# Two states of a Mamba scan take their inputs from GpSimd in SBUF and their decays from ScalarE in PSUM, without PE's transposes

## The chip, the cores and the metric

The kernel runs on one core of one Trainium2 chip. All arithmetic is float32. The metric is the device time of one execution in microseconds; the median of three runs counts, and a shorter time is better. The engines are called as the profile calls them: PE (TensorE matmuls; PEld are its weight loads), DVE (VectorE), ACT (ScalarE), POOL (GpSimd), SP (SyncE, which issues all DMAs here).

## The reference

The input x is (2, 2048, 256). It is normalised, and goes through a Mamba block and a gated feed-forward, each with a residual, then through a mixture of 8 low-rank experts of which the best 2 count. What matters here is the selective scan, with 512 inner channels d, 16 states s and 2048 positions t:

```python
dt = softplus(dt @ dt_proj_w.T + dt_proj_b);  A = -exp(A_log)
def step(h, t):
    dt_t, B_t, C_t, x_t = t
    dA = jnp.exp(dt_t[..., None] * A)
    h = h * dA + dt_t[..., None] * B_t[:, None, :] * x_t[..., None]
    y = jnp.einsum('bds,bs->bd', h, C_t)
    return (h, y)
```

For each state the scan needs a *decay* exp(dt[d,t]·A[d,s]) and an *input* u[d,t]·B[t,s], with u = dt·x. B and C are the same for all channels.

## The kernel before, in words

The sequence is cut into 8 chunks of 256 positions, and there are 2 batches, so the kernel takes 16 *steps* of (chunk, batch). A step passes through five stages, each split in 16 turns: **enter** (norm, input projection, convolution, B and C), **ready** (dt with its softplus, u = dt·x, transposes of u), **main** (the scan), **back** (gate, output projection, feed-forward) and **tail** (router and experts). In one pass of the loop five neighbouring steps are under way at once, each in another stage. The function `drive` writes this order for every engine: for each turn s = 0 to 15, `main(s, n, 0)`, then the turn of the other four stages, then `main(s, n, 1)`. All waits are explicit semaphores; each engine runs its program in order. Steps 0 and 1 have no back or tail beside them, the last one no enter or ready.

Turn s of `main` deals with state s in two halves of 256 channels:

- The input is made with positions on the partitions: `bxT` = uTs · B's column, where B is one scalar per partition. ACT makes it for eleven states (L795), POOL for states 4, 6, 8, 14 and 15 (L561), in a ring of three places, up to three turns ahead. The order of the ring and who must be done with a place are in `ring`, `ring_before` and `made_at`.
- PE turns it by transposes into one of three PSUM banks `psx` (`fill_bx`, L1241), one turn ahead. A bank is free when the scan of three halves earlier is done; the first two fills of the next step are issued in turn 15 of `ready`.
- ACT makes the decay `dA` in SBUF, four exponentials for each state (`decay`, L807), three turns ahead.
- DVE scans (L998): `h` from dA (SBUF) and psx (PSUM), and ACT keeps the last column in `state`.
- POOL multiplies h by C's row, which SP has spread over all partitions in `bC` (L577, `hC`). PE sums hC over the states in `psy`, two turns later, by accumulating transposes (L1260).

Around that, in the other stages: DVE's share of the softplus is L979 and L981 in turn 8 and L985 in turn 9 of `ready`. POOL adds dt (L549) in turn 9 and makes u (L553) in turn 10, in the place of sp_l. In turn 9 of `enter` POOL finishes the convolution (L541), ACT makes xc from it (L708). The second gate (L820) comes in turn 10. The tail's expert sums are the matmuls L1123 from `w_b_sb` into `pst`; turn 14 has sixteen of them in the profile, and DVE adds the result in turn 15 (L1092), between the two halves of state 15's scan. SP stores the expert weights cT and loads them back spread over the partitions (`cbc`), in turn 5 of `tail`; DVE uses them from turn 7 on (L1073).

Of the kernel before, what the change touches and what calls it, by code (L numbers as in the profile page):

```python
# [28 lines left out]
POOL_STATES = (4, 6, 8, 14, 15)  # L29
# [64 lines left out]
def made_at(s):  # L94

    return (-2, -1)[s] if s < 2 else s - 3 if s < S - 1 else S - 3
# [86 lines left out]
def mamba_moe(nc, x, params, w_in, w_x, w_dt, w_out, w_ff, w_fo, w_a, w_b, w_r, bc_scratch, cw_scratch, out):  # L183
# [9 lines left out]
    with ctx:  # L193
# [43 lines left out]
        low = sb("low", [P, T])  # L237
        bc = sb("bc", [2 * S, T])
        sp_e = sb("sp_e", [P, NJ, T])
        sp_l = sb("sp_l", [P, NJ, T])  # L240
        dt = sb("dt", [P, B, NJ, T])
# [35 lines left out]
        cT = sb("cT", [NE, T])  # L277
# [6 lines left out]
        u = sp_l  # L284
        hg = yg
        sk = acc

# [33 lines left out]
        exp_done, scan_done, state_saved = sem("exp_done"), sem("scan_done"), sem("state_saved")  # L321
        hc_done, skip_added, y_summed = sem("hc_done"), sem("skip_added"), sem("y_summed")
# [57 lines left out]
        def _(sp):  # L380
# [23 lines left out]
            def load_c(m, g, multiplied):  # L404

                sp.wait_ge(hc_done, multiplied)
                sp.dma_start(bC[:, g % RINGG], bc_scratch[m[1]][g * G:(g + 1) * G, :].partition_broadcast(P)
                             ).then_inc(c_loaded[g % RINGG], 16)

            def enter(s, m):  # L410
                if s == 7 and not is_last(m):
                    load_x(following(m))
                if s == 13:

                    spread, made = value(count(16 * NG // RINGG, m, -16 * NG // RINGG)), value(count(1, m, 1))
                    for i in range(RINGG):
                        sp.wait_ge(c_loaded[i], spread)
                    sp.wait_ge(bc_done, made)
                    sp.dma_start(bc_scratch[m[1]], bc[S:2 * S, :]).then_inc(bc_stored, 16)
# [28 lines left out]
            def tail(s, m):  # L448
                if s == 5 and not is_last(m):
# [5 lines left out]
                    sp.dma_start(cw_scratch, cT[:, :]).then_inc(cw_stored, 16)  # L455
# [14 lines left out]
        def _(pool):  # L470
# [25 lines left out]
            def norm_again(m):  # L496

                turned, scaled = value(count(len(IN_UNITS), m, 1 - len(IN_UNITS))), value(count(1, m, 1))
                pool.wait_ge(ident_ready, 1)
# [44 lines left out]
            def ready(s, m):  # L544
# [5 lines left out]
                if s == 10:  # L550
                    pool.wait_ge(dt_done, count(1, m, 1))
                    pool.wait_ge(xc_done, count(1, m, 1))
                    nc.gpsimd.tensor_tensor(u[:, :, :], dt[:, b], xc[:, b], ALU.mult).then_inc(u_done, 1)  # L553

            def weigh_u(s, n):
# [4 lines left out]
                pool.wait_ge(bx_filled, count(FILLS, n, HALVES * (ring_before(s) + 1)))  # L560
                nc.gpsimd.tensor_tensor(bxT[:, ring(s)], uTs[:, n[1]],  # L561
                                        BT[:, n[1], :, s:s + 1].to_broadcast([P, SUB, DI]), ALU.mult
                                        ).then_inc(bxT_pool, 1)

            def main(s, n, part):
                if part == 0:
# [81 lines left out]
        def _(act):  # L648
# [70 lines left out]
            def ready(s, m):  # L719
                b = m[1]  # L720
                if s == 0:

                    act.wait_ge(filled_in, in_fill("low", m))
                    nc.scalar.activation(low[:, :], psf[:, 0, :], ACT.Copy).then_inc(low_done, 1)
                if s in (1, 2):

                    i = s - 1
                    act.wait_ge(sp_rest, count(1, m, 0))
                    act.wait_ge(filled_dt, dt_fill(f"dt{i}", m))
# [9 lines left out]
                if s == 6:  # L739

                    act.wait_ge(sp_exp, count(1, m, 1))
                    act.wait_ge(filled_dt, count(len(DT_UNITS), m, 0))
# [18 lines left out]
                if s in (13, 14):  # L761

                    j = s - 13
                    act.wait_ge(bxT_pool, count(len(POOL_STATES), m, -len(POOL_STATES)))
                    act.wait_ge(bxT_act, count(S - len(POOL_STATES), m, len(POOL_STATES) - S))
# [14 lines left out]
            def made(turn, n):  # L780

                for k in range(S):
                    if made_at(k) == turn and k not in POOL_STATES:
                        weigh_u(k, n)
                if turn + 3 < S and not (is_first(n) and turn < -1):
                    decay(turn + 3, n)

            def weigh_u(s, n):
# [4 lines left out]
                act.wait_ge(bx_filled, count(FILLS, n, HALVES * (ring_before(s) + 1)))  # L793
                for j in range(SUB):
                    last = nc.scalar.activation(bxT[:, ring(s), j, :], uTs[:, n[1], j, :], ACT.Copy,  # L795
# [14 lines left out]

            def keep_state(s, n):
# [10 lines left out]
            def main(s, n, part):  # L822
                if part == 0 and s == 3:
# [16 lines left out]
            def back(s, m):  # L840
# [10 lines left out]
                if s == 9:  # L851

                    act.wait_ge(filled_back, back_fill("vT", m))
# [589 lines left out]
```

## Time and profile before

| | |
|---|---|
| runs | 1322.29, 1322.62, 1326.65 us; median 1322.62 |
| profiled execution | 1323.98 us, its span 1322.3 us |
| granted TensorE clock over the span | 0.981 |
| busy | PE 93%, PEld 80%, DVE 76%, ACT 79%, POOL 82% |
| DMA | 74.02 MB, mean 56 GB/s |

The busy shares are means over the whole span; five stages with different needs lie side by side in it. Which engine is waited for has to be read from a stretch of one step. In the rows of the trace "[0.33 <-DVE h]" behind an instruction is the time that its engine was idle before it, and who ended that. Start times are us from the span's start.

### The profile page before, as it was taken

The numbers are of one execution on the slowest core, as the hardware profiler recorded it, in microseconds if no ns is written. First come the engines' busy times: TensorE is split into PE (matmuls) and PEld (weight loads), VectorE is DVE, ScalarE is ACT, GpSimd is POOL, SyncE is SP. The second block draws the span as 40 slices with busy tenths as digits, with TensorE's granted clock in tenths as the row PEclk, the third lists the DMA queues.
The fourth block names the chain that finished last, engine by engine and source line by source line (L and its number), as shares of the span: only waits on it lengthen the run. The fifth ranks groups of instructions, "written<-read, shape, count | busy, mean of one in ns | idle before, by whom it ended". The sixth has DMA issues, their size and how long they took to land.

```text
span 1322.3 us, 24291 instructions
## 1 busy us (share of the span) xinstructions
PE 1230.5 (93%) x7678; PEld 1053.4 (80%) x7678; DVE 1007.8 (76%) x1800; ACT 1039.6 (79%) x2506; POOL 1079.4 (82%) x820
## 2 busy tenths in 40 slices
PE   5677899999999999999999999999999999999988
PEld 3466778887888888788888878888887888887876
DVE  2597969788796977879697797968779796878633
ACT  4989988798787879878797887879788787878521
POOL 2589898998988888888898988889898888889721
PEclk8799999999999999999999999999999999999998
DMA  2411112021121202112111211211111121202010
GB/s 67 177 49 41 49 41 78 21 81 49 33 81 49 78 20 82 48 35 81 51 57 41 75 39 50 81 45 61 41 57 57 50 73 47 66 32 75 17 49 16
DMA packets 29063, 74.02 MB, mean 56 GB/s; under 512 B 3080, under 2 KB 15744, under 8 KB 26496
## 3 DMA queue, kind: packets, MB, share of 16 engines
q1 hardware_dynamic: 28928, 72.35, 16.4%
q8 instruction: 69, 1.13, 0.3%
q14 instruction: 66, 0.54, 0.1%
HBM read 63.56 MB, written 4.58 MB: 52 GB/s over the span
## 4 chain that ended last, share of the span: by engine, by line
PE 61%; DVE 15%; issue 9%; ACT 4%; POOL 2%; DMA 1%; DVEq 0%; SPq 0%; POOLq 0%; ACTq 0%
PE psx L1241 10%; PE psy L1260 10%; PE pst L1123 8%; PE psb L1123 8%; DVE h L998 8%; PE psb L1117 6%; PE psf L1117 4%; PE psf L1209 2%; PE psf L1160 2%; PE psf L1149 2%; PE psb L1215 2%; DVE acc L971 2%; DVE sp_l L985 1%; DVE cbc L1073 1%; PE psx L1117 1%
## 5 line engine op out<-in xcount | busy, mean ns | idle before, releaser
L998 DVE TENSOR_TENSOR_SCAN h<-dA,state,psx 128x256 f32<-128x256 f32 x1024 | 682.6, 726 | 112.4 <-PE psx L1241 96.3
L577 POOL TENSOR_TENSOR hC<-h,bC 128x1024 f32<-128x1024 f32 x256 | 607.0, 2378 | 81.5 <-DVE h L998 74.8
L807 ACT ACTIVATE dA<-dt,neg_a 128x256 f32<-128x256 f32 x1024 | 434.2, 500 | 0.0
L1241 PE MATMUL psx<-ident,bxT 128*128 128x128 f32 x2048 | 306.0, 275 | 29.0 <-DVE h L998 23.8
L1241 PEld LDWEIGHTS psx<-ident,bxT 128*128 128x128 f32 x2048 | 243.9, 142 | 75.5 <-issue 29.3
L795 ACT ACTIVATE bxT<-uTs,BT 128x512 f32<-128x512 f32 x352 | 232.6, 715 | 67.2 <-PE psx L1241 65.7
L1260 PE MATMUL psy<-ident,hC 128*128 128x128 f32 x2048 | 265.5, 273 | 1.4 <-POOL hC L577 1.4
L1260 PEld LDWEIGHTS psy<-ident,hC 128*128 128x128 f32 x2048 | 233.1, 142 | 4.7 <-POOL hC L577 1.7
L561 POOL TENSOR_TENSOR bxT<-uTs,BT 128x1024 f32<-128x1024 f32 x80 | 152.1, 1902 | 24.8 <-PE psx L1241 24.8
L1117 PE MATMUL psb<-nT,w_ff_sb 128*128 128x256 f32 x496 | 121.8, 388 | 15.1 <-ACT yg L820 13.5
L1117 PEld LDWEIGHTS psb<-nT,w_ff_sb 128*128 128x128 f32 x496 | 89.3, 190 | 37.0 <-ACT yg L820 19.7
L1123 PE MATMUL pst<-w_b_sb,cbc 128*128 128x256 f32 x480 | 110.8, 379 | 0.0
L1123 PEld LDWEIGHTS pst<-w_b_sb,cbc 128*128 128x128 f32 x480 | 90.1, 190 | 11.7
L971 DVE SCALAR_TENSOR_TENSOR acc<-psf,par,acc 128x255 f32<-128x255 f32 (+1 forms) x180 | 73.9, 474 | 22.6 <-ACT halo L703 22.6
L1117 PE MATMUL pst<-eT,w_a_sb 128*128 128x256 f32 x336 | 79.4, 379 | 0.0
L492 POOL TENSOR_SCALAR nx<-x,mv,rstd 128x256 f32<-128x256 f32 x60 | 72.9, 1225 | 0.0
L1117 PEld LDWEIGHTS pst<-eT,w_a_sb 128*128 128x128 f32 x336 | 61.7, 190 | 7.2
L1123 PE MATMUL psb<-w_out_sb,yg 128*128 128x256 f32 x256 | 63.6, 393 | 2.0 <-ACT yg L847 2.0
L1117 PE MATMUL psf<-uT,w_in_sb 128*128 128x256 f32 x240 | 60.2, 395 | 3.4 <-DVE acc L971 2.0
L549 POOL TENSOR_TENSOR dt<-dt,sp_l 128x1024 f32<-128x1024 f32 x16 | 37.8, 2364 | 28.0 <-DVE sp_l L985 28.0
L814 ACT ACTIVATE state<-h 128x4 f32<-128x4 f32 x256 | 50.5, 203 | 12.8 <-DVE h L998 12.8
L1123 PE MATMUL psb<-w_fo_sb,yg 128*128 128x256 f32 x256 | 60.4, 379 | 0.0
(168 smaller groups left out, 1641.4 us busy)
## 6 DMA issues: line engine op xcount, KB each, us to landing
bC<-bc_scratch SPq DMA_DIRECT2D x64, 512.0 KB, 3.9
cbc<-cw_scratch SPq DMA_DIRECT2D x15, 1024.0 KB, 4.7
xf<-in_x SPq DMA_DIRECT2D x16, 256.0 KB, 2.7
xk<-xn SPq DMA_DIRECT2D x16, 256.0 KB, 4.3
xb<-in_x SPq DMA_DIRECT2D x16, 256.0 KB, 4.3
out<-x SPq DMA_DIRECT2D x16, 256.0 KB, 2.2
w_in_sb<-in_w_in SPq DMA_DIRECT2D x1, 1024.0 KB, 5.4
w_ff_sb<-in_w_ff SPq DMA_DIRECT2D x1, 1024.0 KB, 5.8
```

What stands on the lines that cost most here:

```text
L492: last = nc.gpsimd.tensor_scalar(dst[:, j, :], src[:, j, :], mv[k][:, j, 0:1], rstd[k + 1][:, j:j + 1], ALU.subtract, ALU.mult)
L561: nc.gpsimd.tensor_tensor(bxT[:, ring(s)], uTs[:, n[1]], BT[:, n[1], :, s:s + 1].to_broadcast([P, SUB, DI]), ALU.mult).then_inc(bxT_pool, 1)
L577: nc.gpsimd.tensor_tensor(hC[:, s % RC], h[:, ring(s)], bC[:, g % RINGG, s % G:s % G + 1, :].to_broadcast([P, NJ, T]), ALU.mult).then_inc( ...
L795: last = nc.scalar.activation(bxT[:, ring(s), j, :], uTs[:, n[1], j, :], ACT.Copy, scale=BT[:, n[1], j, s:s + 1])
L807: last = nc.scalar.activation(dA[:, s % RA, j, :], dt[:, n[1], j, :], ACT.Exp, scale=neg_a[:, j, s:s + 1])
L814: nc.scalar.activation(state[:, n[1], :, s:s + 1], h[:, ring(s), :, T - 1:T], ACT.Copy).then_inc(state_saved, 1)
L971: nc.vector.scalar_tensor_tensor(out=acc[:, j, tap:], in0=x_bank(i, m)[:, j % 2, 0:T - tap], scalar=pcol(C_CONVW + j * TAPS + k), in1=acc[ ...
L998: last = nc.vector.tensor_tensor_scan(h[:, r, j, :], dA[:, s % RA, j, :], psx[bx_bank(fill)][:, k, :], state[:, b, j, s:s + 1], ALU.mult, ...
L1117: last = mm(dst[:, i, :], w[:, k, c:c + P], rhs[:, k, :], start=k == 0, stop=k == kt - 1)
L1123: last = mm(dst[:, j, :], lhs[:, k, j * P:(j + 1) * P], w[:, k, :], start=k == 0, stop=k == kt - 1)
L1241: last = nc.tensor.transpose(psx[bx_bank(fill)][:, k, j * P:(j + 1) * P], bxT[:, ring(s), j, c:c + P], ident[:, :])
L1260: last = mm(psy[j][:, i * P:(i + 1) * P], hC[:, s % RC, i, j * P:(j + 1) * P], ident[:, :], is_transpose=True, start=False, stop=s == S - ...
```

## The change

States 14 and 15 are called `DIRECT`. For them nothing is turned. POOL multiplies u (channels on the partitions) by B's row, spread over all partitions like C's, and leaves the input in SBUF. ACT writes the exponentials into the `psx` banks that PE filled before, in two groups of two for each state, and the scan reads its decays from PSUM and its inputs from SBUF. The order of POOL's products changes: those for 14 and 15 stand in turns 8 and 10 (`weigh_direct`), not in turns 11 and 13. SP stores B together with C in DRAM and loads the two rows in turn 5.

Places: the input of state 14 is made in `ygt`, that of state 15 in `sp_e`, B's rows lie in `un`; `u` gets a tile of its own in place of sp_l's; `low` and `cT` lie in the dead `nT`. Each of these sharings comes with waits, at the head of the instruction that writes the place. `bxT` now has fourteen states, so its ring is simply s % 3, and the first two bxT of a step need state 12's and 13's transposes only. In the diff, cut to its core, come the shared helpers and places, then SP, POOL (`norm_again`, `ready`, `weigh_u`, `weigh_direct`, `main`), ACT, DVE and PE.

```diff
-POOL_STATES = (4, 6, 8, 14, 15)
+DIRECT = (14, 15)
+POOL_STATES = (4, 6, 8)
+TURNED = HALVES * (S - ND)
...
-    return (-2, -1)[s] if s < 2 else s - 3 if s < S - 1 else S - 3
+    return (-2, -1)[s] if s < 2 else s - 3
...
+def turned_before(s):
+    return s - RX if s >= RX else (12, 13, 11)[s] - S
...
+def turned(s):
+    return HALVES * (s + 1) if s >= 0 else HALVES * (s + S + 1) - TURNED
...
-        u = sp_l
+        low = nT[:, 0, :]
+        cT = nT[0:NE, 1, :]
+        bB = un
+        def direct_inputs(s):
+            return (ygt[:, :, :].rearrange("p j (k t) -> p (j k) t", t=T), sp_e[:, :, :])[DIRECT.index(s)]
...
+                if part == 0 and s == 5:
+                    gone = value(count(len(IN_UNITS), n, 1 if is_late(n) else 2 * len(IN_UNITS) + 1))
+                    sp.wait_ge(filled_in, gone)
+                    sp.dma_start(bB[:, :, :], bc_scratch[n[1]][DIRECT[0]:DIRECT[0] + ND, :].partition_broadcast(P)
+                                 ).then_inc(b_loaded, 16)
...
+                pool.wait_ge(direct_done, weighed)
...
+                    pool.wait_ge(filled_dt, count(len(DT_UNITS), m, 0))
+                    pool.wait_ge(direct_done, count(ND, m, 0))
...
-                pool.wait_ge(bx_filled, count(FILLS, n, HALVES * (ring_before(s) + 1)))
+                pool.wait_ge(bx_filled, count(TURNED, n, turned(turned_before(s))))
+            def weigh_direct(i, n):
+                if i == 0:
+                    pool.wait_ge(b_loaded, count(16, n, 16))
+                    pool.wait_ge(u_done, count(1, n, 1))
+                    pool.wait_ge(filled_back, count(len(BACK_UNITS), n, 2 - len(BACK_UNITS)))
+                else:
+                    pool.wait_ge(sp_rest, count(1, n, 1 if is_last(n) else 2))
+                nc.gpsimd.tensor_tensor(direct_inputs(DIRECT[i]), u[:, :, :],
+                                        bB[:, i:i + 1, :].to_broadcast([P, NJ, T]), ALU.mult).then_inc(direct_done, 1)
             def main(s, n, part):
+                if part == 0 and s in (8, 10):
+                    weigh_direct((8, 10).index(s), n)
...
+            def decay_direct(s, part, n):
+                fill = HALVES * s + part
+                act.wait_ge(scan_done, count(FILLS, n, bx_before(fill) + 1))
+                for k in range(PAIR):
+                    j = PAIR * part + k
+                    last = nc.scalar.activation(psx[bx_bank(fill)][:, k, :], dt[:, n[1], j, :], ACT.Exp,
+                                                scale=neg_a[:, j, s:s + 1])
+                last.then_inc(direct_exp, 1)
             def main(s, n, part):
+                if s + 1 in DIRECT:
+                    decay_direct(s + 1, part, n)
...
+                if s in DIRECT:
+                    dve.wait_ge(direct_exp, count(HALVES * ND, n, fill - TURNED + 1))
...
+                    decays, inputs = ((in_psum, direct_inputs(s)[:, j, :]) if s in DIRECT
+                                      else (dA[:, s % RA, j, :], in_psum))
...
             def main(s, n, part):
-                if s + 1 < S:
+                if s + 1 < S - ND:
                     fill_bx(s + 1, part, n)
```

On PE, turns 12 to 15 of a steady step (psx0 to psx2 are the three banks; `MATMUL psy<-ident,hC` is the sum over states) are before:

```order
L1241 MATMUL psx1<-ident,bxT 128x128 x4
L1223 MATMUL psf<-ident,sp_l 128x128 x4
...
L1241 MATMUL psx2<-ident,bxT 128x128 x4
...
L1241 MATMUL psx0<-ident,bxT 128x128 x4
L1123 MATMUL pst<-w_b_sb,cbc 128x256 x8
...
L1241 MATMUL psx1<-ident,bxT 128x128 x4
...
L1241 MATMUL psx0<-ident,bxT 128x128 x4
L1241 MATMUL psx1<-ident,bxT 128x128 x4
L1160 MATMUL psf<-xc,w_x_sb 128x256 x4
```

And in the changed kernel the same stretch reads:

```order
L1300 MATMUL psf<-ident,u 128x128 x4
L1200 MATMUL psb<-w_fo_sb,yg 128x256 x4
L1200 MATMUL pst<-w_b_sb,cbc 128x256 x4
...
L1200 MATMUL pst<-w_b_sb,cbc 128x256 x8
...
L1318 MATMUL psx0<-ident,bxT 128x128 x4
L1318 MATMUL psx1<-ident,bxT 128x128 x4
L1237 MATMUL psf<-xc,w_x_sb 128x256 x4
```

Four psx groups are gone: three ahead of the end of the expert matmuls (`w_b_sb`, x8), one behind them. The last two psx groups are the next step's state 0.

On POOL, turns 7 to 10 of a steady step (`nx` is the back stage's norm, the hC are those of states 7, 8, 9 and 10) are before:

```order
L492 TENSOR_SCALAR nx<-x1,mv1,rstd2 128x256 x2
...
L577 TENSOR_TENSOR hC<-h,bC 128x1024
...
L577 TENSOR_TENSOR hC<-h,bC 128x1024
...
L549 TENSOR_TENSOR dt<-dt,sp_l 128x1024
...
L541 TENSOR_TENSOR acc<-acc,edge 128x4x3
...
L577 TENSOR_TENSOR hC<-h,bC 128x1024
L553 TENSOR_TENSOR sp_l<-dt,xc 128x1024
...
L577 TENSOR_TENSOR hC<-h,bC 128x1024
...
L561 TENSOR_TENSOR bxT<-uTs,BT 128x1024
```

And in the changed kernel:

```order
L626 TENSOR_TENSOR hC<-h,bC 128x1024
...
L609 TENSOR_TENSOR ygt<-u,un 128x1024
...
L626 TENSOR_TENSOR hC<-h,bC 128x1024
...
L583 TENSOR_TENSOR dt<-dt,sp_l 128x1024
...
L575 TENSOR_TENSOR acc<-acc,edge 128x4x3
...
L626 TENSOR_TENSOR hC<-h,bC 128x1024
L609 TENSOR_TENSOR sp_e<-u,un 128x1024
...
L589 TENSOR_TENSOR u<-dt,xc 128x1024
```

The product for state 14 (into ygt) now stands between the hC of state 7 and that of state 8, the one for state 15 (into sp_e) between the hC of state 9 and u; the bxT that stood behind the hC of state 10 is gone.

## Rows read from the trace of the kernel before

**Rows 1.** The page: busy time, the chain that ended last; and all of L1092.

```profile
PE 1230.5 (93%) x7678; PEld 1053.4 (80%) x7678; DVE 1007.8 (76%) x1800; ACT 1039.6 (79%) x2506; POOL 1079.4 (82%) x820
...
PE 61%; DVE 15%; issue 9%; ACT 4%; POOL 2%; DMA 1%; DVEq 0%; SPq 0%; POOLq 0%; ACTq 0%
...
L1092 DVE TENSOR_TENSOR x<-x,pst x15: 686/689/689, 263.9 to 1297.5; 128x512 f32<-128x512 f32 x15
```

**Rows 2.** PE in order of time, one steady step: start us, us, instruction.

```profile
705.27 1.99 PE L1117 MATMUL psb<-nT,w_ff_sb 128*128 128x256 f32 x8 [0.90 <-ACT yg L820]
...
725.21 0.60 PE L1241 MATMUL psx<-ident,bxT 128*128 128x128 f32 x4
725.64 3.62 PE L1123 MATMUL pst<-w_b_sb,cbc 128*128 128x256 f32 x16
729.10 0.60 PE L1241 MATMUL psx<-ident,bxT 128*128 128x128 f32 x4
...
731.34 0.66 PE L1241 MATMUL psx<-ident,bxT 128*128 128x128 f32 x4 [0.33 <-DVE h L998]
```

**Rows 3.** DVE in order of time, the same step.

```profile
691.75 2.66 DVE L979 SCALAR_TENSOR_TENSOR sp_l<-sp_l,ln_one,sp_e 128x1024 f32<-128x1024 f32 x1
694.34 0.68 DVE L981 TENSOR_SCALAR sp_e<-sp_e 128x1024 f32<-128x1024 f32 x1
...
698.09 1.90 DVE L985 TENSOR_TENSOR sp_l<-sp_l,sp_e 128x1024 f32<-128x1024 f32 x1
...
718.90 2.69 DVE L998 TENSOR_TENSOR_SCAN h<-dA,state,psx 128x256 f32<-128x256 f32 x4 [2.82 <-PE psx L1241]
...
729.30 0.69 DVE L1092 TENSOR_TENSOR x<-x,pst 128x512 f32<-128x512 f32 x1 [2.07 <-PE pst L1123]
729.90 3.93 DVE L998 TENSOR_TENSOR_SCAN h<-dA,state,psx 128x256 f32<-128x256 f32 x6
```

**Rows 4.** POOL in order of time, the same step.

```profile
690.97 2.37 POOL L577 TENSOR_TENSOR hC<-h,bC 128x1024 f32<-128x1024 f32 x1
696.55 2.36 POOL L577 TENSOR_TENSOR hC<-h,bC 128x1024 f32<-128x1024 f32 x1 [3.21 <-DVE h L998]
700.07 2.36 POOL L549 TENSOR_TENSOR dt<-dt,sp_l 128x1024 f32<-128x1024 f32 x1 [1.17 <-DVE sp_l L985]
702.39 0.21 POOL L541 TENSOR_TENSOR acc<-acc,edge 128x12 f32<-128x12 f32 x1
```

**Rows 5.** All of L979 and of L985: duration ns min/median/max, first and last start.

```profile
L979 DVE SCALAR_TENSOR_TENSOR sp_l<-sp_l,ln_one,sp_e x16: 1265/2662/2915, 33.2 to 1152.1; 128x1024 f32<-128x1024 f32 x16
...
L985 DVE TENSOR_TENSOR sp_l<-sp_l,sp_e x16: 1224/1899/3150, 35.1 to 1158.7; 128x1024 f32<-128x1024 f32 x16
```

**Rows 6.** Groups by line and form, 300 to 1100 us: busy us, mean ns of one.

```profile
L807 ACT ACTIVATE dA<-dt,neg_a 128x256 f32<-128x256 f32 x662 | 280.8, 500 | 0.0
...
L561 POOL TENSOR_TENSOR bxT<-uTs,BT 128x1024 f32<-128x1024 f32 x51 | 96.9, 1901 | 17.3 <-PE psx L1241 17.3
```

**Rows 7.** ACT in order of time, the same step as rows 2.

```profile
720.64 0.60 ACT L768 ACTIVATE uTs<-psf 128x512 f32<-128x512 f32 x1 [2.75 <-PE psf L1223]
...
729.74 2.56 ACT L795 ACTIVATE bxT<-uTs,BT 128x512 f32<-128x512 f32 x4 [4.97 <-PE psx L1241]
```

**Rows 8.** DVE, then POOL, in order of time, in step 1.

```profile
152.83 1.26 DVE L979 SCALAR_TENSOR_TENSOR sp_l<-sp_l,ln_one,sp_e 128x1024 f32<-128x1024 f32 x1
154.00 0.69 DVE L981 TENSOR_SCALAR sp_e<-sp_e 128x1024 f32<-128x1024 f32 x1
...
153.13 6.12 POOL L577 TENSOR_TENSOR hC<-h,bC 128x1024 f32<-128x1024 f32 x2
```

**Rows 9.** cbc: its load's issue and landing, and DVE's first use of it.

```profile
L459 SPq DMA_DIRECT2D cbc<-cw_scratch x1: 331/331/331, 681.0 to 681.0; - x1
...
DMA to landing us min/median/max: 4.9/4.9/4.9
...
687.25 0.67 DVE L1073 TENSOR_TENSOR cbc<-cbc,pst 128x512 f32<-128x512 f32 x1
```

More of the change, by code:

```diff
@@ L723, in ready @@
                     act.wait_ge(filled_in, in_fill("low", m))
-                    nc.scalar.activation(low[:, :], psf[:, 0, :], ACT.Copy).then_inc(low_done, 1)
+                    act.wait_ge(filled_back, count(len(BACK_UNITS), m, -2 * len(BACK_UNITS) - 1))
+                    act.wait_ge(cw_stored, count(16, m, -48))
+                    nc.scalar.activation(low, psf[:, 0, :], ACT.Copy).then_inc(low_done, 1)
                 if s in (1, 2):
@@ L780, in made @@
             def made(turn, n):
-                for k in range(S):
+                for k in range(S - ND):
                     if made_at(k) == turn and k not in POOL_STATES:
                         weigh_u(k, n)
-                if turn + 3 < S and not (is_first(n) and turn < -1):
+                if turn + 3 < S - ND and not (is_first(n) and turn < -1):
                     decay(turn + 3, n)
@@ L792, in weigh_u @@
                     act.wait_ge(uTs_done, count(2, n, 2))
-                act.wait_ge(bx_filled, count(FILLS, n, HALVES * (ring_before(s) + 1)))
+                act.wait_ge(bx_filled, count(TURNED, n, turned(turned_before(s))))
                 for j in range(SUB):
-                    last = nc.scalar.activation(bxT[:, ring(s), j, :], uTs[:, n[1], j, :], ACT.Copy,
+                    last = nc.scalar.activation(bxT[:, s % RX, j, :], uTs[:, n[1], j, :], ACT.Copy,
                                                 scale=BT[:, n[1], j, s:s + 1])
@@ L988, in main @@
                 b, r = n[1], ring(s)
+                fill = HALVES * s + part
                 if part == 0:
-                    dve.wait_ge(exp_done, count(S, n, s + 1))
+                    if s in DIRECT:
+                        dve.wait_ge(direct_done, count(ND, n, s - DIRECT[0] + 1))
+                    else:
+                        dve.wait_ge(exp_done, count(S - ND, n, s + 1))
                     dve.wait_ge(hc_done, count(S, n, ring_before(s) + 1))
                     dve.wait_ge(state_saved, count(S, n, ring_before(s) + 1))
-                fill = HALVES * s + part
-                dve.wait_ge(bx_filled, count(FILLS, n, fill + 1))
+                if s in DIRECT:
+                    dve.wait_ge(direct_exp, count(HALVES * ND, n, fill - TURNED + 1))
+                else:
+                    dve.wait_ge(bx_filled, count(TURNED, n, fill + 1))
                 for k in range(PAIR):
                     j = PAIR * part + k
-                    last = nc.vector.tensor_tensor_scan(h[:, r, j, :], dA[:, s % RA, j, :], psx[bx_bank(fill)][:, k, :],
-                                                        state[:, b, j, s:s + 1], ALU.mult, ALU.add)
+                    in_psum = psx[bx_bank(fill)][:, k, :]
+                    decays, inputs = ((in_psum, direct_inputs(s)[:, j, :]) if s in DIRECT
+                                      else (dA[:, s % RA, j, :], in_psum))
+                    last = nc.vector.tensor_tensor_scan(h[:, r, j, :], decays, inputs, state[:, b, j, s:s + 1],
+                                                        ALU.mult, ALU.add)
                 last.then_inc(scan_done, 1)
@@ L1208, in step_sizes @@
                     j = 2 * i + k
-                    last = mm(size_bank(i, m)[:, k, :], w_dt_sb[:, j * P:(j + 1) * P], low[:, :], start=True, stop=True)
+                    last = mm(size_bank(i, m)[:, k, :], w_dt_sb[:, j * P:(j + 1) * P], low, start=True, stop=True)
                 return last
```

38 lines of the change are left out of this document (24 added, 14 removed).

## The prediction

> **What bounds the kernel now.** I began with the page. PE is busy 93% of the span and holds 61% of the chain that ended last, VectorE (DVE) 15% and "issue" 9% [rows 1]. So PE time is worth something, but only where PE's end is waited for. The count of the tail's last addition (L1092: 15, of which 14 in the scheduled loop) tells how many of the 16 steps carry the full load of all stages [rows 1].
>
> Then I read one steady step in order of time, engine by engine. Its stretch at states 12 to 15 is PE's: PE resumes at 705.27 after the gate, and from there no row of it has a wait until 731.34. There it waits 0.33 us for a scan [rows 2]. DVE has nothing to do for 2.07 us before L1092, because that takes the sixteen expert matmuls that PE starts at 725.64. The second half of state 15's scan stands behind L1092 in DVE's program and starts at 729.90; bank psx1 is free for the next step's second fill (731.34) only when it is done [rows 2, 3].
>
> Earlier in the same step the path is DVE's and GpSimd's (POOL): softplus L979, L981, two pairs of scans, L985, which POOL's dt addition awaits (1.17 us idle at 700.07), then acc, ScalarE's xc and silus, the second gate, and PE, which waits 0.90 at 705.27 [rows 2 to 4]. Whatever delays L985 delays PE one for one. The rows also show something that is no semaphore: L979 takes 1265 ns at best and 2662 in the median, L985 1224 and 1899 [rows 5]. Both read two tiles from SBUF. In the steady step POOL's product runs 690.97 to 693.33 and L979 ends 1.08 later, at 694.41; the product at 696.55 ends at 698.91 and L985 1.08 later, at 699.99 [rows 3, 4]. So such a DVE instruction does nothing until POOL's running product is over, and then takes its 1.08. The scans (one input in PSUM) pass beside POOL's products.
>
> **The change, part by part.** *PE.* Four groups of four transposes per step go; the third and the last are the rows at 725.21 and 729.10. Each takes 0.43 to 0.44, by the distance to the next row (725.21 to 725.64) [rows 2]. Three stand ahead of the expert matmuls' end, so L1092 starts at 729.30 - 1.30 = 728.0, the last scan pair is over at about 729.95, and the next step's second fill goes at 730.04 in place of 731.34. The fourth gives nothing: PE waits 0.33 for that scan even now, and would wait 0.44 longer. **Gain 1.30 us per full step.**
>
> *ScalarE.* Eight exponentials (states 14 and 15, four column blocks each) move from dA to psx, in four groups of two; the count stays. None of before writes PSUM, so the price is bounded by the neighbours: 280.8 us for 662 from SBUF to SBUF, hence 0.42 each, or 0.50 if nothing of one overlapped the next [rows 6]. I take 0.42. Three groups (2.5 us) now stand behind the first uTs copy; the engine idles 2.75 before the second copy and 4.97 before its bxT pair at 729.74 [rows 7]. Laying the new order out with each group's wait (the first for the scan of state 12, the third for the first pair of the scans from 718.90, over at 720.2 [rows 3]) I get state 13's copy at 725.5, the scan of state 15 from 725.6 to 727.0, and L1092 not before 728.0: 1.0 us of cover. At 0.50 each it still holds. Without the cover, each 0.1 us would be 1.4 us in all. The 4.97 goes away altogether, since bxT for states 1 and 2 no longer waits for state 15's transposes. That is worth nothing on this path, as PE's second fill waits for the scan.
>
> *Scans of 14 and 15* swap which input is in PSUM. Still one in each memory; I take the same 0.65 us. A tenth more on the two behind L1092 would be 0.2 per step, 3 us in all.
>
> *GpSimd.* bxT for 14 and 15 (1.90 each [rows 6]) goes; two products of the hC form (2.37) come: +0.94 per step on an engine that is idle here and there. The second one, after hC(9), pushes u and hC(10) back 2.4, and the missing bxT(14) gives 1.9 of it back; readers are 4 us and more away. Its DVE neighbours are scans, or read PSUM. **The first one is what matters.** It stands right behind hC(7), with its semaphores long met, so it is ready at 693.33, when until now POOL was idle for 3.21 us until 696.55 [rows 4]. L979 is at that moment waiting for the same end.
>
> Who goes first? No row has two POOL products back to back against a waiting DVE instruction. The nearest is the reverse, in step 1 [rows 8]: L979 starts at 152.83 unhindered, POOL's product is issued at 153.13, DVE's L981 at 154.00 also takes its best time, and the two products take 6.12 instead of 2 x 2.36 = 4.72. So the product began 1.4 late, at 154.53, after *both* DVE instructions. DVE is not overtaken in its own run. I take this reading: L979 gets in at 693.33 and ends at 694.41 as now, L981 follows, the new product works from 694.34 + 0.53 = 694.87 to 697.24. hC(8), now from 696.55, goes from there to 699.60, and L985 ends at 700.68 instead of 699.99. **Loss 0.69 us per step that has a softplus.** By the other bound the POOL product goes first (rival 1, loss 2.37); below, no loss at all.
>
> The Trainium skill (SBUF — State Buffer, "Who interferes with whom") says that a VectorE instruction with two SBUF inputs and a GpSimd one that reads SBUF exclude each other, and that issue order decides which of them is blocked. L979's blocked rows agree with the first half. By the second half L979, issued first, would go first, which gives the same 0.69; yet in step 1 the later L981 went ahead of an earlier product, so these rows do not settle the order.
>
> *DMA and SP.* bB adds 256 KB per step between a bC load and the store of the expert weights. cbc is issued at 681.00, lands 4.9 later at 685.9, and is first used at 687.25: cover 1.35 [rows 9]. A bC load of 512 KB takes 3.9 and cbc's 1024 KB takes 4.9, so by the difference 256 KB more is 0.5 us at most; half a bC load, 1.95, is the other bound, and 0.6 of it would show. I take nothing. SP itself is idle there. The other new waits (low and cT in nT, u on its own, un before bB) ask for work that ended a stage or a step before.
>
> **Sum.** 13 steps have both (L979 stands 16 times, of which the first is the opening and two are the light steps 0 and 1): 13 x (1.30 - 0.69) = 7.9. The last step has only the gain: 1.3. Steps 0 and 1 have no expert matmuls, PE does not bound them: only the loss, 2 x 0.69 = 1.4. Net 7.8 us. The profiled execution took 1323.98 (its span is 1322.3), so it would be 1316.2; the median of the runs is 1322.62, 1.4 lower, and I predict 1322.6 - 7.8 = **1314.8**.
>
> **Rivals.** 1. *POOL keeps its port over two products* (slower). L979 then waits until 695.70, everything to L985 moves by 2.37, hC(8) with it. Per step 2.37 - 1.30 = 1.07: 13 x 1.07 - 1.3 + 2 x 2.37 = 17.3, hence 1340. For it: step 1's rows show a holder keeping the port over two instructions, and POOL's successive rows overlap (700.07 + 2.36 against 702.39) just as DVE's do. Against it: L979 has waited 1.6 us by then. It decides as soon as the loss per step passes 1.30.
> 2. *The softplus loses nothing* (a gap, or the new product lands in the idle 3.21 after all): 14 x 1.30 = 18.2, hence 1304.
> 3. *cbc or an exponential into PSUM comes late*, 0.6 per step: the net is about nothing, 1322.5.
> 4. *The transposes were not bounding*: no gain and a loss of 0.69 in 15 steps, 1333. The unbroken PE rows from 705.27 speak against it.
>
> **Chances.** My forecast 0.46, rival 1 0.27, rival 2 0.12, rival 3 0.09, rival 4 0.06. Rivals 2 and 1 have to be inside for 8 in 10: 1303 to 1340. The forecast alone spans 1309 to 1319. About 0.3% (4 us) is what a measurement of this kernel can tell from no change. Faster than 1318.6: most of the forecast and rival 2, 0.55. Within: 0.14. Slower than 1326.6: rivals 1 and 4, 0.31.
>
> **What the new profile would show.** Right: in the steady step no psx matmuls between the UT transposes and the next step's fills; L1092 to the next step's second fill as now (2.04 us); a POOL product right behind hC(7), and L979 at 2.66 with L985 at about 2.6. Rival 1: L979 at 5.0, and each step 1.07 us longer. Rival 2: both as before, and each step 1.3 us shorter. Rival 3: DVE idle before the first cbc product, released by a DMA, or before state 15's scan, released by ScalarE. I would be wrong above all if DVE and POOL trade the port in an order other than step 1 suggests.

## The result, and the profile after

The changed kernel takes 1361.97 us (median of 4 runs, 1359.54 to 1363.96), the kernel before 1324.21 beside it (median of 4, 1322.29 to 1326.65). The ratio is 1.0283, with an interval of 1.0254 to 1.0313. It is slower by about 38 us. I had forecast 1314.8, some 8 us faster than before, and a range of 1303 to 1340; the result lies outside it, on the other side.

The page of the changed kernel, the lines that answer to [rows 1]: busy time, the chain that ended last, and two groups of instructions.

```profile
span 1362.0 us, 24154 instructions
...
PE 1226.9 (90%) x7422; PEld 1045.2 (77%) x7422; DVE 1035.8 (76%) x1800; ACT 1040.4 (76%) x2506; POOL 1109.2 (81%) x820
...
PE 57%; DVE 14%; issue 7%; ACT 3%; DMA 2%; POOL 1%; DVEq 1%; SPq 0%; ACTq 0%; POOLq 0%
...
L859 ACT ACTIVATE dA<-dt,neg_a 128x256 f32<-128x256 f32 x896 | 380.1, 500 | 0.0
...
L870 ACT ACTIVATE psx<-dt,neg_a 128x256 f32<-128x256 f32 x128 | 55.4, 463 | 65.5 <-DVE h L1075 65.5
```

PE has 256 instructions fewer and is busy 3.6 us less in a span that is 40 us longer. The 256 transposes that are gone would have taken some 28 us by the 0.43 to 0.44 of a group of four, so the rest of its work takes longer in sum. It waits, and it runs at a lower clock. Where that is, shows in a steady step. It begins at DVE's row at 706.14 and lasts 79.50; the one of before lasts 77.15 (681.42 to 758.57). These are DVE's rows, which answer to [rows 3] (L1047 was L979, L1049 was L981, L1053 was L985, the scans L998):

```profile
716.48 2.68 DVE L1047 SCALAR_TENSOR_TENSOR sp_l<-sp_l,ln_one,sp_e 128x1024 f32<-128x1024 f32 x1
719.09 2.84 DVE L1049 TENSOR_SCALAR sp_e<-sp_e 128x1024 f32<-128x1024 f32 x1
721.85 2.65 DVE L1075 TENSOR_TENSOR_SCAN h<-dA,state,psx 128x256 f32<-128x256 f32 x4
...
725.00 1.89 DVE L1053 TENSOR_TENSOR sp_l<-sp_l,sp_e 128x1024 f32<-128x1024 f32 x1
```

And POOL's, which answer to [rows 4]; L609 is the new product:

```profile
715.70 2.39 POOL L626 TENSOR_TENSOR hC<-h,bC 128x1024 f32<-128x1024 f32 x1
718.03 3.35 POOL L609 TENSOR_TENSOR ygt<-u,un 128x1024 f32<-128x1024 f32 x1
723.45 2.36 POOL L626 TENSOR_TENSOR hC<-h,bC 128x1024 f32<-128x1024 f32 x1 [2.08 <-DVE h L1075]
```

L1047 waits for hC(7), takes its 1.08 and ends at 719.16, all as before. The new product, issued at 718.03, gets its turn when L1047 is over (it is 3.35 long, 1.0 of it waiting) and ends at 721.38. L1049 was issued at 719.09 and stands behind it: 2.84 in place of 0.68, though it reads only one tile from SBUF. The scans start 2.2 later than before. L1053 is not slower than before. Over all steps, by line (duration ns min/median/max, first and last start):

```profile
L1049 DVE TENSOR_SCALAR sp_e<-sp_e x16: 685/2844/2867, 33.4 to 1192.5; 128x1024 f32<-128x1024 f32 x16
```

The mean of L1049 is 2576 ns, which is two times 0.69 us and fourteen times 2.84: the first in the opening and the one of step 1 are spared. What comes of it on PE, in order of time:

```profile
719.65 1.04 PE L1337 MATMUL psy<-ident,hC 128*128 128x128 f32 x8
723.27 0.66 PE L1318 MATMUL psx<-ident,bxT 128*128 128x128 f32 x4 [2.59 <-DVE h L1075]
723.86 0.29 PE L1266 MATMUL psf<-ident,bc 16*128 16x16 f32 x2
724.08 2.94 PE L1194 MATMUL psb<-nT,w_ff_sb 128*128 128x256 f32 x8
726.81 2.68 PE L1194 MATMUL pst<-eT,w_a_sb 128*128 128x256 f32 x8
...
733.65 1.99 PE L1194 MATMUL psb<-nT,w_ff_sb 128*128 128x256 f32 x8 [0.69 <-ACT yg L883]
...
752.71 3.62 PE L1200 MATMUL pst<-w_b_sb,cbc 128*128 128x256 f32 x16
```

PE stands still for 2.59 us (0.42 in the step of before), and its next two groups of eight take 2.94 and 2.68, where such groups take 1.99 and 1.89 at full clock. The windows of the same kernel (length, busy us and instructions of each engine, granted clock, DMA share, GB/s) say why:

```profile
719.00:724.00 5.00, 2.41 (x20) 1.93 (x18) 5.00 (x6) 0.92 (x3) 2.92 (x2) 1.00 0.48 157
724.00:729.00 5.00, 5.00 (x17) 4.10 (x17) 5.00 (x7) 4.78 (x10) 3.84 (x2) 0.66 0.01 3
729.00:745.00 16.00, 15.31 (x96) 12.72 (x95) 11.13 (x21) 10.97 (x24) 15.04 (x9) 1.00 0.09 30
```

The granted clock falls soon behind the idle time to 1.2 GHz, half its speed: 0.66 as the mean of 5 us is 3.4 us at half (5 - 0.5 x 3.4 = 3.3). The kernel before is at clock 1.00 from 200 to 1190 us, and no idle time of PE's there is longer than 1.2 us; this one falls in nine of the eleven steps that start from 302 to 1103. PE resumes after the gate at 733.65, 27.51 after the step's start; before it was 705.27, 23.85 after [rows 2]. That is 3.66 lost. From there to the sixteen expert matmuls it takes 19.06, and before 725.64 - 705.27 = 20.37 [rows 2]: 1.31 won. From there to the end the steps agree within 0.01. 3.66 - 1.31 = 2.35 is the growth of this step (79.50 - 77.15).

Two steps of the changed kernel have no fall of the clock, 866.27 to 944.28 and 944.28 to 1022.30. They last 78.01: 77.15 + 2.17 - 1.30 = 78.02. So there are three terms: 1.30 won on PE, 2.17 lost on the port, and what the clock takes, 1.5 in the step above (79.50 - 78.01), more in others. (In the kernel before, the three steps that start at 447.18, 602.77 and 758.57 last 78.42, 78.65 and 78.22, some 1.2 longer than their neighbours; the kernel with the filler below has three such steps as well, with no fall of the clock. They are left out of these comparisons.)

### The profile page after: what moved, and what is told of

Same layout as the page of the kernel before. It is cut to its first block, busy times and chain, and to the rows that moved or that the text cites. A ratio compares the mean times of both kernels' runs of the same rounds, so it can differ in the third digit from the quotient of the medians.

```text
span 1362.0 us, 24154 instructions
## 1 busy us (share of the span) xinstructions
PE 1226.9 (90%) x7422; PEld 1045.2 (77%) x7422; DVE 1035.8 (76%) x1800; ACT 1040.4 (76%) x2506; POOL 1109.2 (81%) x820
## 4 chain that ended last, share of the span: by engine, by line
PE 57%; DVE 14%; issue 7%; ACT 3%; DMA 2%; POOL 1%; DVEq 1%; SPq 0%; ACTq 0%; POOLq 0%
PE psy L1337 9%; PE psb L1194 8%; PE psx L1318 8%; PE pst L1200 8%; PE psb L1200 7%; DVE h L1075 7%; PE psf L1194 3%; DVE sp_e L1049 3%; PE pst L1194 2%; PE psf L1286 2%; PE psf L1237 2%; PE psf L1226 2%; PE psb L1292 2%; DMA cbc<-cw_scratch 1%; DVE acc L1039 1%
## 5 line engine op out<-in xcount | busy, mean ns | idle before, releaser
L1075 DVE TENSOR_TENSOR_SCAN h<-dA,state,psx 128x256 f32<-128x256 f32 x896 | 596.9, 726 | 105.1 <-PE psx L1318 96.4
L859 ACT ACTIVATE dA<-dt,neg_a 128x256 f32<-128x256 f32 x896 | 380.1, 500 | 0.0
L1318 PE MATMUL psx<-ident,bxT 128*128 128x128 f32 x1792 | 273.2, 280 | 69.3 <-DVE h L1075 59.0
L1318 PEld LDWEIGHTS psx<-ident,bxT 128*128 128x128 f32 x1792 | 216.6, 144 | 112.8 <-DVE h L1075 45.3
L1194 PE MATMUL psb<-nT,w_ff_sb 128*128 128x256 f32 x496 | 137.1, 425 | 14.9 <-ACT yg L883 13.8
L1194 PEld LDWEIGHTS psb<-nT,w_ff_sb 128*128 128x128 f32 x496 | 98.8, 209 | 40.1 <-ACT yg L883 19.8
L870 ACT ACTIVATE psx<-dt,neg_a 128x256 f32<-128x256 f32 x128 | 55.4, 463 | 65.5 <-DVE h L1075 65.5
L597 POOL TENSOR_TENSOR bxT<-uTs,BT 128x1024 f32<-128x1024 f32 x48 | 91.3, 1901 | 6.3 <-PE psx L1318 6.3
L1194 PE MATMUL pst<-eT,w_a_sb 128*128 128x256 f32 x336 | 85.1, 399 | 0.0
L1106 DVE TENSOR_TENSOR yg<-yg,psb 128x512 f32<-128x512 f32 x31 | 21.3, 688 | 60.9 <-PE psb L1194 60.9
```

The costliest lines, as they stand in the source:

```text
L597: nc.gpsimd.tensor_tensor(bxT[:, s % RX], uTs[:, n[1]], BT[:, n[1], :, s:s + 1].to_broadcast([P, SUB, DI]), ALU.mult).then_inc(bxT_pool, 1)
L859: last = nc.scalar.activation(dA[:, s % RA, j, :], dt[:, n[1], j, :], ACT.Exp, scale=neg_a[:, j, s:s + 1])
L870: last = nc.scalar.activation(psx[bx_bank(fill)][:, k, :], dt[:, n[1], j, :], ACT.Exp, scale=neg_a[:, j, s:s + 1])
L1075: last = nc.vector.tensor_tensor_scan(h[:, r, j, :], decays, inputs, state[:, b, j, s:s + 1], ALU.mult, ALU.add)
L1194: last = mm(dst[:, i, :], w[:, k, c:c + P], rhs[:, k, :], start=k == 0, stop=k == kt - 1)
L1318: last = nc.tensor.transpose(psx[bx_bank(fill)][:, k, j * P:(j + 1) * P], bxT[:, s % RX, j, c:c + P], ident[:, :])
```

## The experiments

The times of the kernel before were 1322.29 (median of 7) beside the kernels with both products in turn 10, with one more product, with the filler and with state 15's scan as a whole, and 1323.43 (median of 7) beside the other four. Line numbers in rows are those of each kernel, shifted by a few. "..." in an edit stands for what is left out of it.

**Both products in one place.** The first product leaves turn 8 and goes right behind hC(9), ahead of the second one.

```
-                if part == 0 and s in (8, 10):
-                    weigh_direct((8, 10).index(s), n)
+                if part == 0 and s == 10:
+                    weigh_direct(0, n)
+                    weigh_direct(1, n)
```

> The changed kernel with the product for state 14 moved from turn 8 to turn 10, so that both new products stand together behind the scan product of state 9, where VectorE has no instruction with two SBUF inputs. Nothing is left out. Theory 1 (the port and what follows from it): the whole loss comes from VectorE's L981, which waits for the new product in turn 8, and from PE's lower clock after the idle stretch that this makes. Then L981 is back at 0.68 us, PE's clock stays at its upper level in the steady steps, the gain of 1.30 us in 14 steps is left, and the time is 1304 to 1308 us. Theory 2 (the new places and their waits, the exponentials written into PSUM, or the added load of B's rows are to blame): these are all still there, and the time stays above 1340.

Measured: 1309.71 us, ratio 0.9892 (0.9868 to 0.9917), 2 us above the upper end of the first theory and 30 below the other's bound. Everything of the change is there but the place of one POOL instruction, and the kernel is some 50 us faster for it. Its DVE rows, in the same place of a step, and L1050 (the second softplus instruction) over all steps:

```profile
686.32 2.68 DVE L1048 SCALAR_TENSOR_TENSOR sp_l<-sp_l,ln_one,sp_e 128x1024 f32<-128x1024 f32 x1
688.92 0.68 DVE L1050 TENSOR_SCALAR sp_e<-sp_e 128x1024 f32<-128x1024 f32 x1
...
L1050 DVE TENSOR_SCALAR sp_e<-sp_e x16: 679/681/686, 33.5 to 1141.8; 128x1024 f32<-128x1024 f32 x16
```

Its steady step lasts 75.86 (675.98 to 751.84), that is 77.15 - 1.30 within 0.01, the gain as I had it. ScalarE's exponentials into PSUM, the swapped scans, bB's load and the shared tiles are all in it and cost nothing that shows in this step. In the ten steps 3 to 12 it wins 13.3 us; the rest of the profiled execution gives 4.7 of that back (below). That execution was the slowest of four, 1315.60 us at a mean clock of 0.976; the fastest took 1306.56 at 0.984.

**One more product, nothing else.** The kernel before, with a POOL product of the same size in turn 8 whose result nobody reads. (VectorE waits for it in turn 2 of the back stage, before it writes ygt itself.)

```
+                if part == 0 and s == 8:
+                    pool.wait_ge(filled_back, count(len(BACK_UNITS), n, 2 - len(BACK_UNITS)))
+                    nc.gpsimd.tensor_tensor(ygt[:, :, :].rearrange("p j (k t) -> p (j k) t", t=T), dt[:, n[1]], dt[:, n[1]],
+                                            ALU.mult).then_inc(extra_done, 1)
...
+                    dve.wait_ge(extra_done, count(1, m, 1))
```

> The kernel before with one product of 128 x 1024 on GpSimd put in turn 8 between the products of states 7 and 8, the square of dt into the free tile ygt; nothing reads it, all else is as before. Theory 1: this alone makes L981 take 2.84 us in place of 0.68, 2.17 us in each of 15 steps (33 us), and PE's clock falls in most steps behind it as in the changed kernel (some 25 us more): 1370 to 1385 us. Theory 2: GpSimd is idle there for 3.2 us, so the product costs nothing or a few us: below 1335.

Measured: 1357.23 us, ratio 1.0248 (1.0217 to 1.0278). The product alone makes the kernel before as slow as the change does, within 5 us. The expectation was 13 to 28 us too high, for the port's part because this product, with one input tile, works 1.9 us and not 2.3, and L986 (L981 of before) waits 1.70 for it; the clock's part came out at 7 and not 25 (the fourth experiment shows it).

```profile
L986 DVE TENSOR_SCALAR sp_e<-sp_e x16: 681/2378/2380, 34.0 to 1190.7; 128x1024 f32<-128x1024 f32 x16
```

**The clock alone.** The changed kernel, with 22 transposes of the identity on PE at the end of turn 8, in the idle time, into a bank that is free there.

```
+                    if s == 8 and not is_last(n):
+                        pe.wait_ge(z1_copied, count(1, n, 2))
+                        for i in range(FILLER):
+                            nc.tensor.transpose(psf[:, 0, 0:P], ident[:, :], ident[:, :])
```

> The changed kernel with 22 transposes of the identity on PE (0.11 us each, into a part of psf that is free) at the end of turn 8, where PE is idle for 2.6 us until the scan of state 8; nothing reads them. Theory 1: PE's clock no longer falls behind that stretch, the steps of 79.4 to 82.2 us become steps of 78.0 and the time is 1332 to 1342; L981 is still at 2.84. If the slow matmuls behind the idle stretch have another cause than the clock, the time stays at 1362. If the filler itself delays the transposes behind it, 1362 or more.

Measured: 1345.26 us, ratio 1.0161 (1.0137 to 1.0185), 3 us above the upper end. More PE work makes the changed kernel some 17 us faster (1361.97 - 1345.26). PE, in order of time:

```profile
708.33 2.57 PE L1356 MATMUL psf<-ident 128*128 128x128 f32 x22
711.10 0.66 PE L1319 MATMUL psx<-ident,bxT 128*128 128x128 f32 x4 [0.20 <-DVE h L1076]
711.68 0.29 PE L1267 MATMUL psf<-ident,bc 16*128 16x16 f32 x2
711.91 1.99 PE L1195 MATMUL psb<-nT,w_ff_sb 128*128 128x256 f32 x8
713.74 1.89 PE L1195 MATMUL pst<-eT,w_a_sb 128*128 128x256 f32 x8
```

L1050 waits as ever (2854 ns in the median), and the two groups behind take 1.99 and 1.89 again. The windows 200 to 600, 600 to 1000 and 1000 to 1190 us are at clock 1.00 here, and at 0.97, 0.99 and 0.97 in the changed kernel. The steady step lasts 78.03, just as the changed kernel's two steps without a fall. This parts the loss: some 17 us are the clock's. The other 23 (1345.26 against 1322.29) are what the wait for the port costs, less the gain. The rows of full steps account for about half of them: 14 x 2.17 - 14 x 1.30 = 12.2, an estimate. Where the other 11 lie stands under "The parts of the span"; what makes them is not shown.

**Product and filler on the kernel before.** The second experiment with the third's transposes.

> Kernel before with one GpSimd product more in turn 8, as in the earlier experiment, and 22 idle transposes on PE in the same turn, which keep PE from standing still. Theory (port about 1.7 to 2.2 us per step, the clock what is beyond that): steps of 78.9 to 79.3 us with no stretch at half clock, in all 1346 to 1353, so 5 to 10 under the same kernel without the transposes. Rival (the product costs PE time by itself and not through a wait): no less than 1357.

Measured: 1349.83 us, ratio 1.0197 (1.0179 to 1.0214), as expected, and the clock is 1.00 from 200 to 1190 us. The steady step lasts 78.87, which is 77.15 + 1.72, and L987 waits 1.70. So the parting holds on either kernel: the wait in DVE's queue moves the step by its own length, and the clock comes on top, here with 7.4 us (1357.23 - 1349.83).

**State 15's scan as a whole ahead of the tail's last addition**, on the kernel with both products in turn 10. This tests the other end of the path. There the two fills of the next step start 1.38 apart (723.24 and 724.62) where one follows the other in 0.44 when nothing holds it; can the 0.94 between be had too?

```
+                if s < S - 1:
+                    scan(s, n, part)
+                elif part == 0:
+                    scan(s, n, 0)
+                    scan(s, n, 1)
```

> As the first of these kernels (both new products in turn 10), and VectorE scans both halves of state 15 ahead of the tail's last addition L1169 instead of one on each side of it; nothing is left out. In the kernel before this order could bring nothing, because the second half's transposes came behind the expert matmuls. Theory: PE's second fill of the next step then no longer waits for that addition, which gives back the fourth group of transposes and the wait behind it, 0.8 to 0.9 us per step: 1290 to 1296 us. Rival: VectorE's later additions and scans only move and PE waits elsewhere; the time is that of the first kernel, 1304 to 1308.

Measured: 1303.73 us, ratio 0.9852 (0.9833 to 0.9872), the best of all. But a step is only 0.28 shorter (75.57), so the theory's 0.8 to 0.9 failed, and the time is at the lower end of the rival's. PE's rows show both halves of it:

```profile
721.77 1.04 PE L1326 MATMUL psx<-ident,bxT 128*128 128x128 f32 x8
...
738.03 0.63 PE L1416 MATMUL psb<-ident,ygt 128*128 128x128 f32 x4 [0.67 <-issue]
```

The next step's two fills go in one piece, with no wait (in the kernel with both products in turn 10 it is 0.77), and 16 us later PE waits 0.67 for the transposes of ygt, where that kernel has no wait of as much as 0.6 at that place. Some 0.9 won, some 0.7 given back. What ended that wait the profile does not say; I did not follow it further.

**The softplus without its second instruction.** Both kernels leave out the addition of 1.0 and -1.0 to sp_e (L981, now L1049), so the softplus goes without its correction for rounding and its values change. There is then no instruction right behind L979 that needs the port. First the kernel before, as the control:

```
-                    nc.vector.tensor_scalar(sp_e[:, :, :], sp_e[:, :, :], 1.0, -1.0, ALU.add, ALU.add
-                                            ).then_inc(sp_fix, 1)
```

The signal that it gave goes with L979 now.

> Kernel before with VectorE's second softplus instruction (L981) left out, so the softplus is rounded otherwise: a control for the next kernel. Both theories: the scans behind it start 0.68 us earlier in each of 15 steps and that path sets PE's gate wait, so about 10 us less than the kernel before, 1310 to 1318.

Measured: 1314.36 us, ratio 0.9932 (0.9910 to 0.9954). Then the changed kernel with the same line out:

> Changed kernel with VectorE's second softplus instruction (L1049) left out: there is then nothing on VectorE for the new GpSimd product to overtake. Theory (the port is handed over after each instruction, and the loss sits in L1049's wait): the scans start as in the control, PE has no wait of 2.6 us and its clock does not fall, only hC(8) and L1053 come about 0.8 later, and the 1.30 of each step stay: control - 18 + 12, so 5 us under the control, 1303 to 1313. Rival (the 2.2 us of a step come from something else of the change, such as the waits of ScalarE or the shared buffers): 20 to 40 us above the control.

Measured: 1313.37 us, ratio 0.9923 (0.9902 to 0.9944), 1 us under the control (5 were expected; it is 0.4 above the range) and 49 under the changed kernel. One VectorE instruction of 0.68 us less is worth 49 us. The steady step is 75.88 against the control's 76.58. That is 0.70 won, and not 1.30, so 0.60 of the gain is lost again, since the product now delays hC(8), and with it the last softplus instruction (median 2556 ns against 1895):

```profile
L1052 DVE TENSOR_TENSOR sp_l<-sp_l,sp_e x16: 1224/2556/3144, 33.4 to 1145.9; 128x1024 f32<-128x1024 f32 x16
```

That is the loss that I had predicted for the change, 0.69 per step, and here it measures 0.66 on the instruction and 0.60 on the step. It is real, but only where L981 does not exist.

**The product in two halves**, each 128x512, at the same place of the changed kernel.

```
-                nc.gpsimd.tensor_tensor(direct_inputs(DIRECT[i]), u[:, :, :],
-                                        bB[:, i:i + 1, :].to_broadcast([P, NJ, T]), ALU.mult).then_inc(direct_done, 1)
+                for k in ((0, 2), (2, NJ)) if i == 0 else ((0, NJ),):
+                    last = nc.gpsimd.tensor_tensor(direct_inputs(DIRECT[i])[:, k[0]:k[1], :], u[:, k[0]:k[1], :],
+                                                   bB[:, i:i + 1, :].to_broadcast([P, k[1] - k[0], T]), ALU.mult)
+                last.then_inc(direct_done, 1)
```

> Changed kernel with state 14's product written as two GpSimd instructions of half the size, at the same place. Theory (one instruction each in turn): L1049 waits for the first half alone, about 1.2 us in place of 2.17, a step lasts 77.15 + 1.1 - 1.3 = 76.95 where the clock does not fall, and the time is 1320 to 1335, by how often it still falls. Rival (GpSimd keeps the port as long as it has work queued, and the time of both halves stands ahead of L1049): as the changed kernel, 1358 to 1366.

Measured: 1333.27 us, ratio 1.0073 (1.0054 to 1.0093). DVE, then POOL, in order of time, and all of L1051:

```profile
696.73 2.67 DVE L1049 SCALAR_TENSOR_TENSOR sp_l<-sp_l,ln_one,sp_e 128x1024 f32<-128x1024 f32 x1
699.33 1.76 DVE L1051 TENSOR_SCALAR sp_e<-sp_e 128x1024 f32<-128x1024 f32 x1
...
698.29 3.92 POOL L610 TENSOR_TENSOR ygt<-u,un 128x512 f32<-128x512 f32 x2
...
L1051 DVE TENSOR_SCALAR sp_e<-sp_e x16: 680/1760/1769, 33.3 to 1159.3; 128x1024 f32<-128x1024 f32 x16
```

L1051 waits for one half: 1.76 and not 2.84, though the other half was queued on POOL. The two halves take 3.92, some 1.5 longer than their work, because the first waits for L1049 and the second for L1051. Here the engines take turns, one instruction each. The step is 76.93, as expected (76.95), and the clock is 1.00 from 200 to 1190 us: with a wait 1.08 shorter it does not fall.

**The parts of the span.** The start of each step is DVE's row of L1014 (L1091 after); step 1 is counted from the first such row, at 143.7 in the kernel before. From those rows of the profiled executions, in us:

```
                        to step 1  steps 1-2  steps 3-12  steps 13-15  rest   span
before                    143.7      149.3      774.9       203.4      51.0  1322.3
after                     147.1      154.9      801.1       211.4      47.6  1362.0
after, filler             146.6      154.1      785.0       206.4      51.0  1343.1
after, halves             144.9      154.0      773.3       208.0      47.7  1327.9
after, both in turn 10    145.6      148.8      761.6       206.7      51.0  1313.7
same, scan 15 whole       146.8      148.2      757.7       198.9      50.4  1302.0
```

Every version in this table needs 1 to 3.5 us more up to step 1 than the kernel before (but so does the one with only the product added, 2.9), and most need some us more in the last steps and the rest. There the clock falls in all kernels, at times that differ from one to the next (0.84 from 1190 to 1220 us with both products in turn 10, 0.94 before). In the kernel with the filler the surplus of steps 1 and 2 is 4.8 and that of steps 13 to 15 is 3.0, where the waits and gains of their rows give less than 1 each.

Two things in these parts come with the change. In step 1 PE waits 4.40 for ScalarE's bxT, at 193.75 in the changed kernel (4.41 at 188.96 with both products in turn 10); the kernel before has waits of 1.44 and 0.56 there. And in the last steps VectorE waits longer for cbc's load: these are its first two such waits in the kernel before, then in the one with both products in turn 10.

```profile
1148.38 0.69 DVE L1073 TENSOR_TENSOR cbc<-cbc,pst 128x512 f32<-128x512 f32 x1 [2.07 <-DMA cbc<-cw_scratch]
1219.46 0.69 DVE L1073 TENSOR_TENSOR cbc<-cbc,pst 128x512 f32<-128x512 f32 x1 [2.15 <-DMA cbc<-cw_scratch]
...
1136.37 0.69 DVE L1151 TENSOR_TENSOR cbc<-cbc,pst 128x512 f32<-128x512 f32 x1 [3.35 <-DMA cbc<-cw_scratch]
1206.84 0.69 DVE L1151 TENSOR_TENSOR cbc<-cbc,pst 128x512 f32<-128x512 f32 x1 [3.61 <-DMA cbc<-cw_scratch]
```

What either costs in time no run shows.

## Why the prediction was wrong

**What bounds the kernel: right.** PE with its gate wait, the softplus path ahead of it and the scan of state 15 behind it were the places where the time changed. Each shift of the softplus path that leaves the clock alone moved the step nearly one for one (2.17, 1.70 and 1.08 of wait). At the scan's end it is not so: of the 0.94 there a step got 0.28.

**The gain of 1.30 per full step: right to 0.01**, in the changed kernel (1.31 in the step above) and alone with both products in turn 10 (75.85). The fourth group gave nothing, as I had it: L1169 to the next step's second fill is 2.05, and 2.04 before. In the last step, where I had it too, it did not show.

**ScalarE, scans, GpSimd's second product, DMA at nothing: right in the full steps.** The exponentials into PSUM take 0.46 as the profile counts them, against 0.50 for those into SBUF, and a pair of them occupies 0.86; scans with decays in PSUM take 723 and 735 ns in the mean against 726; the scan of state 15 waits 0.92 per step for ScalarE's copy of the state, and L1169's own wait of 0.71 stands behind it, which is the cover that I had put at 1.0. All of it together is in the 1309.71. Rivals 3 and 4 are ruled out by that run's full steps, which are 1.30 shorter. In the last steps cbc does come later, by 1.3 and 1.5 us, as rival 3 had it.

**The loss of 0.69: the step that failed.** "DVE is not overtaken in its own run. I take this reading: L979 gets in at 693.33 and ends at 694.41 as now, L981 follows." L979 did get in. L981 (now L1049) did not follow: the product came between, and the loss was 2.17 on the scans and not 0.69 on L985. That is a wrong order on the port, and with it a wrong size of the loss per step; it turns the forecast gain into a loss by itself. I had taken step 1's order [rows 8], where L981 passed a waiting product, for a property of DVE. The changed kernel has both orders: in step 1 L1049 again goes ahead of a product that has waited since 156.48,

```profile
156.17 1.26 DVE L1047 SCALAR_TENSOR_TENSOR sp_l<-sp_l,ln_one,sp_e 128x1024 f32<-128x1024 f32 x1
157.35 0.69 DVE L1049 TENSOR_SCALAR sp_e<-sp_e 128x1024 f32<-128x1024 f32 x1
...
156.48 3.79 POOL L626 TENSOR_TENSOR hC<-h,bC 128x1024 f32<-128x1024 f32 x1
```

and in the fourteen others it does not. Step 1 is the case in which L1047 itself had not waited; that this is what decides is not shown. The rows of the steady step were of the other kind, and I weighed one odd row above them. The order that holds in these steps, one instruction each in turn, was none of my readings. Of the instructions that wait for a product I had named only those that read two tiles, L979 and L985; L981, which reads one, waits as well. Rival 1 was nearer in size (2.37) and wrong in kind: GpSimd does not keep the port from L979.

The Trainium skill (SBUF — State Buffer, "Who interferes with whom") says that issue order decides who is blocked. Followed from instruction to instruction that gives what the steady step shows: L1047 (716.48) ahead of the product (718.03), and the product ahead of L1049 (719.09). I had applied it to L979 alone, and called it the same 0.69. Step 1 still speaks against it: the product issued at 156.48 came after L1049, issued at 157.35.

**What was missing: the clock.** Even with 2.17 in place of 0.69, my own sum gives 13 x (2.17 - 1.30) - 1.3 + 2 x 2.17 = 14.3, so 1337, inside the range. The kernel with the filler is at 1345; these 8 us (10 with step 1's wait taken out of the sum, since it was spared) are in the parts that I did not take apart. The 17 from there to 1362 are TensorE at half clock behind its idle time of 2.6 us. The sum had no term for it: I had counted a wait on PE as its own length. The profile of before holds no such idle time in the steady stretch and hence no fall, but its page does show the clock at 0.7 to 0.8 in the opening, where PE waits most. I read it and did not ask what a longer wait would do.

## What to carry to other kernels

In the steady steps here, a product put into an idle gap of GpSimd landed between two VectorE instructions, since it was ready while the first of them held or awaited the port; ask of each VectorE instruction near the new place, and not only of the first, what will stand ahead of it. Where the order of grants isn't known, measure it with one product that nobody reads, at the place in question: it cost 35 us here, with nothing else changed. And a wait on PE can have two prices, its length and the clock behind it; filling the wait with idle transposes shows whether the second is paid.

## What the runs showed of the hardware that I had not expected

In the steady steps the two engines alternate after single instructions, also where the holder has its next one queued (halves: 1.76, then 3.92). And an instruction with a single SBUF tile is held up as well: L1049, 0.68 by itself, took 2.84 beside the product. There are exceptions on both sides. Step 1 above is one. The other: in the kernel before with product and filler, twice of sixteen times L985 (L979 of before) waited for two products, as in rival 1:

```profile
228.31 5.26 DVE L985 SCALAR_TENSOR_TENSOR sp_l<-sp_l,ln_one,sp_e 128x1024 f32<-128x1024 f32 x1
233.49 0.68 DVE L987 TENSOR_SCALAR sp_e<-sp_e 128x1024 f32<-128x1024 f32 x1
...
228.25 2.38 POOL L583 TENSOR_TENSOR hC<-h,bC 128x1024 f32<-128x1024 f32 x1
230.58 1.91 POOL L570 TENSOR_TENSOR ygt<-dt 128x1024 f32<-128x1024 f32 x1
```

In both cases (the other is 1174.66 behind 1174.56) it was issued within 0.1 us of the first product, and in the steady step 0.8 behind it. What the rule is stays open; no run here varied that distance by itself. A tensor_scalar of GpSimd's was beside L1047 in step 1 (nx, 154.09 to 156.48, L1047 1.26 from 156.17) with no delay that shows; but the two overlap by 0.3 us only, which settles little.

The clock fell in nine steps of eleven, behind an idle time of 2.6 us (2.0 in the last of them), but not behind a like one in the other two:

```profile
883.41 0.66 PE L1318 MATMUL psx<-ident,bxT 128*128 128x128 f32 x4 [2.60 <-DVE h L1075]
...
884.22 1.99 PE L1194 MATMUL psb<-nT,w_ff_sb 128*128 128x256 f32 x8
```

It did not fall behind the 1.5 us of the kernel with halves, and there not behind one of 3.05 us at 238.24 either. So the length of one idle time does not decide it alone. What does is open here. Even the transposes of an identity, with no use but to be there, bought 17 us.
